# Ahead of layer 2 of a cross network: the second filter is loaded by SyncE and made into parts by VectorE, ScalarE does more of the first tile's stores and loads

## The reference

```python
for W in filters:                       # three layers, 128 outputs each
    b, f, d = x0.shape
    g = xk.shape[1]
    z = jnp.einsum('bfd,bgd->bfgd', x0, xk).reshape(b, f * g, d)
    cur = jnp.einsum('bpd,pm->bmd', z, W)
    outs.append(cur)
    xk = cur
result = jnp.concatenate(outs, axis=1)
z = jnp.sum(result, axis=-1)            # (512, 384)
h = jnp.concatenate([z, dense_ctx], axis=1)
h = jnp.maximum(h @ W_top1 + b_top1, 0.0)
h = jnp.maximum(h @ W_top2 + b_top2, 0.0)
y = h @ W_top3
```

## Time and profile before

| | us |
|---|---|
| median of 3 runs | 685.78 (683.43 to 687.0) |
| the profiled execution | 684.99 |
| its span in the profile | 683.0 |
| layer 2 of tile 0 begins, from the span's start | 48.48 |

### The profile page before, as it was taken

How to read it: one execution, slowest core, us unless ns; L and a number is a source line. 1 busy time by engine, 2 the same in 40 slices (tenths; PEclk the granted TensorE clock), 3 DMA queues, 4 the chain that set the end, 5 groups by cost and what they waited for, 6 DMA issues and landing times.

```text
span 683.0 us, 11480 instructions
## 1 busy us (share of the span) xinstructions
PE 642.6 (94%) x2942; PEld 510.8 (75%) x2942; DVE 564.9 (83%) x1914; ACT 383.4 (56%) x1157; POOL 532.2 (78%) x528
## 2 busy tenths in 40 slices
PE   3279999999999999999999999999999999999998
PEld 1156777767768787888868787888878888888867
DVE  4459897988989897989879897989879797988760
ACT  0447574746657574747467474746557474655431
POOL 6756989898999899897879989897959988574420
PEclk9989999999999999999999999999999999999998
DMA  9536533104040404013130404004040221200000
GB/s 185 92 93 232 151 74 92 30 8 116 10 116 8 116 9 116 6 26 98 31 94 6 116 9 110 13 8 115 7 115 7 63 62 36 82 1 1 1 1 0
DMA packets 70979, 41.92 MB, mean 61 GB/s; under 512 B 45889, under 2 KB 55761, under 8 KB 70786
## 3 DMA queue, kind: packets, MB, share of 16 engines
q1 hardware_dynamic: 58286, 35.53, 19.5%
q10 hardware_dynamic: 7380, 4.38, 3.1%
q0 software_dynamic: 5248, 1.29, 1.9%
HBM read 39.20 MB, written 1.94 MB: 60 GB/s over the span
## 4 chain that ended last, share of the span: by engine, by line
PE 73%; DVE 12%; issue 7%; POOL 3%; SPq 2%; ACT 2%; DMA 1%; DVEq 0%; POOLq 0%
PE y L853 18%; PE y L855 16%; PE y L854 16%; DVE scaled L756 10%; PE late L871 4%; PE side L860 4%; PE acc L835 3%; PE acc L829 3%; PE acc L830 3%; PE y L871 2%; ACT scaled L560 1%; PE late L882 1%; SPq L376 1%; POOL z_parts L463 1%; DVE z L717 1%
## 5 line engine op out<-in xcount | busy, mean ns | idle before, releaser
L756 DVE SCALAR_TENSOR_TENSOR scaled<-y,x_rows,scaled 128x128 f32<-128x128 f32 x1728 | 466.4, 343 | 71.2 <-ACT scaled L560 41.9
L560 ACT ACTIVATE scaled<-y,x_rows 128x128 f32<-128x128 f32 x768 | 218.3, 366 | 216.2 <-PE y L855 200.7
L853 PE MATMUL y<-w_hi,x_parts 128*128 128x512 f32 (+1 forms) x640 | 276.8, 432 | 6.8 <-DVE scaled L756 3.2
L855 PE MATMUL y<-w_hi,x_parts 128*128 128x512 f32 (+1 forms) x640 | 248.1, 388 | 0.0
L854 PE MATMUL y<-w_lo,x_parts 128*128 128x512 f32 (+1 forms) x640 | 247.4, 387 | 0.0
L463 POOL TENSOR_TENSOR z_parts<-z,z_parts 117x512 fp32r<-117x512 f32 (+1 forms) x107 | 138.4, 1294 | 33.4 <-ACT z_parts L514 32.5
L452 POOL DMA_INDIRECT emb_quads<-in_small_tables_dram,quad_rows x144 | 138.8, 964 | 27.2 <-issue 15.3
L853 PEld LDWEIGHTS y<-w_hi,x_parts 128*128 128x128 f32 x640 | 120.5, 188 | 44.7 <-DVE scaled L756 19.3
L855 PEld LDWEIGHTS y<-w_hi,x_parts 128*128 128x128 f32 x640 | 120.1, 188 | 25.0
L854 PEld LDWEIGHTS y<-w_lo,x_parts 128*128 128x128 f32 x640 | 121.0, 189 | 18.2
L478 POOL TENSOR_TENSOR sum<-sum,scaled 128x512 f32<-128x512 f32 x63 | 81.6, 1295 | 29.1 <-DVE scaled L756 28.3
(11 more groups left out here) (95 smaller groups left out, 360.2 us busy)
## 6 DMA issues: line engine op xcount, KB each, us to landing
z<-x_turned SPq DMA_DIRECT2D x311, 78.0 KB
x_three<-x_turned SPq DMA_DIRECT2D x48, 78.0 KB
x_turned<-emb_quads SPq DMA_DIRECT2D x156, 8.0 KB
w_sb<-in_w_dram SPq DMA_DIRECT2D x1, 2496.0 KB
emb_quads<-in_small_tables_dram,quad_rows POOLq DMA_INDIRECT x144
s_sb<-in_w_dram ACTq DMA_DIRECT2D x12, 160.0 KB
x_turned<-emb_singles SPq DMA_DIRECT2D x89, 2.0 KB
x_turned<-emb_quads SPq DMA_DIRECT2D x64, 2.0 KB
```

Of the source, the lines that this page charges most:

```text
L560: done = act.activation(scaled[:, k % 2, BY_ACT.index(j), i * M:(i + 1) * M], y2[n % RING][:, i * M:(i + 1) * M], ACT.Copy, scale=x0_rows[ ...
L756: dve.scalar_tensor_tensor(part, y2[n % RING][:, i * M:(i + 1) * M], x0_f, part, ALU.mult, ALU.add).then_inc(terms_in, 1)
L853: pe.matmul(dst, x1_hi[:, t % 2, cols], hi, start=True, stop=False)
L855: pe.matmul(dst, x1_lo[:, t % 2, cols], hi, start=False, stop=True).then_inc(y_ready, 1)
```

## The change

The edits all stand ahead of layer 2 of tile 0.

1. SyncE issues the 16 DMAs of the second filter, right behind its three loads of ids and numbers. Before, ScalarE issued them.
2. VectorE makes the second filter's high part itself, piece by piece, ahead of each low part. Before, ScalarE made it.
3. The stores of tile 0 are shared out anew. SyncE keeps 13 DMAs (five singles, quads 8, 4, 7, 0 and 5 in copy 0). ScalarE has the others of tile 0, and the six of tile 1's singles come first.
4. ScalarE issues `three` and chunks 0, 1, 2 and 4 of tile 0. SyncE issues chunks 3, 5 and 6 and `three_blocks`. Before, ScalarE had chunks 0, 3 and 5.
5. ScalarE's four activations on the dense part move from behind w0_hi to between the high parts of chunks 1 to 4. `three` is now a function of any queue, and ScalarE's copy is called `three_to_psum`.

```diff
--- before.py
+++ after.py
@@ -376,15 +376,22 @@
                     queue.dma_start(x0_dram[u, at:at + n, :].rearrange("f (b d) -> (f b) d", d=D),
                                     emb_quads[SPT * j:SPT * (j + n), u % 2, i, :]).then_inc(stored[u % 2], 16)
 
+        def three(queue, u):
+            if u >= 2:
+                queue.wait_ge(three_up, u - 1)
+                queue.wait_ge(rows_t, u - 1)
+            for r in range(3):
+                queue.dma_start(x0_three[F * r:F * r + F, u % 2, :], x0_dram[u, 0:F, :]).then_inc(three_in[u % 2], 16)
+
         block = ctx.enter_context(nc.Block())
 
         @block.sync
         def _(sp):
-            def stores(u, copies):
-                if u != 1:
-                    store_singles(sp, u, copies)
+            def stores(u):
+                if u > 1:
+                    store_singles(sp, u, (0, 1))
                 for i in QUAD_ORDER:
-                    store_quad(sp, u, i, copies)
+                    store_quad(sp, u, i, (0, 1))
 
             def three_blocks(u):
 
@@ -393,21 +400,22 @@
                 for k in range(3):
                     sp.dma_start(x0_stack[F * k:F * k + F, u % 2, :], x0_dram[u, 0:F, P * k:P * k + P]).then_inc(stack_in[u % 2], 16)
 
-            def three(u):
-                if u >= 2:
-                    sp.wait_ge(three_up, u - 1)
-                    sp.wait_ge(rows_t, u - 1)
-                for r in range(3):
-                    sp.dma_start(x0_three[F * r:F * r + F, u % 2, :], x0_dram[u, 0:F, :]).then_inc(three_in[u % 2], 16)
-
             sp.dma_start(ids_sb[:, 0, :], ids[0:P, :]).then_inc(ids_in, 16)
             sp.dma_start(table_number[:, 0, :], row_numbers[0:1, 0:SMALL].to_broadcast([P, SMALL])).then_inc(numbers_in, 16)
             sp.dma_start(ids_sb[:, 1:GROUPS, :], ids[P:B, :].rearrange("(g p) f -> p g f", p=P)).then_inc(rest_ids_in, 16)
+            for j in range(W1_PIECES):
+                load_filter(sp, j)
+            store_singles(sp, 0, (0,))
+            for i in (8, 4, 7, 0, 5):
+                store_quad(sp, 0, i, (0,))
             for u in range(TILES):
-                stores(u, (0,) if u == 0 else (0, 1))
-                sp.wait_ge(stored[u % 2], 16 * STORES * (u // 2 + 1))
-                three(u)
-                for c in (1, 2, 4, 6) if u == 0 else range(C0):
+                if u > 0:
+                    stores(u)
+                    sp.wait_ge(stored[u % 2], 16 * STORES * (u // 2 + 1))
+                    three(sp, u)
+                else:
+                    sp.wait_ge(stored[0], 16 * STORES)
+                for c in (3, 5, 6) if u == 0 else range(C0):
                     if u > 0:
                         n = C0 * (u - 1) + c
                         if low_by_dve(n):
@@ -530,7 +538,10 @@
                 act.activation(diag[at, t % 2, :, b, :], x0_rows[at, t % 2, :, :], ACT.Copy,
                                scale=mask_sb[at, b:b + 1]).then_inc(diag_in, 1)
 
-            def three(u):
+            def dense_part(c):
+                act.activation(dense_h1[:, c, :], y2[c][:, 0:LEFT], ACT.Identity, bias=bt1_sb[:, c:c + 1]).then_inc(dense_up, 1)
+
+            def three_to_psum(u):
                 act.wait_ge(three_in[u % 2], 48 * (u // 2 + 1))
                 if u > 0:
                     act.wait_ge(prod, C0 * u)
@@ -611,31 +622,26 @@
             act.dma_start(wt1_sb[0:16, 3, :], wt1[3 * P:FEATURES, :]).then_inc(dense_in, 16)
             act.dma_start(dense_sb[:, :], dense_t).then_inc(dense_in, 16)
             act.dma_start(bt1_sb[:, :], bt1).then_inc(dense_in, 16)
-            for j in range(W1_PIECES):
-                load_filter(act, j)
             act.wait_ge(w0_sum, 1)
             copy(w0_hi[:, :, :], w0_raw).then_inc(w0_hi_in, 1)
+            store_singles(act, 0, (1,))
+            store_singles(act, 1, (0, 1))
+            for i, copies in ((4, (1,)), (0, (1,)), (1, (0, 1)), (2, (0, 1)), (3, (0, 1)), (6, (0,))):
+                store_quad(act, 0, i, copies)
+            act.wait_ge(stored[0], 16 * STORES)
+            three(act, 0)
+            turned_rows(act, 0, 0)
+            turned_rows(act, 0, 1)
+            three_to_psum(0)
+            turned_rows(act, 0, 2)
             act.wait_ge(dense_in, 48)
             act.wait_ge(dense_ready, 1)
-            for c in range(H1 // P):
-                act.activation(dense_h1[:, c, :], y2[c][:, 0:LEFT], ACT.Identity, bias=bt1_sb[:, c:c + 1]).then_inc(dense_up, 1)
-            store_singles(act, 0, (1,))
-            for i in QUAD_ORDER:
-                if any(len(rows) > 1 for _, _, _, rows in runs(QUADS[i])):
-                    store_quad(act, 0, i, (1,))
-                if i == 0:
-                    store_singles(act, 1, (0, 1))
-            for j in range(W1_PIECES):
-                act.wait_ge(w1_in[j], 64)
-                copy(w1_hi[:, j:F:4, :], w1_raw[:, j:F:4, :]).then_inc(w1_hi_in, 1)
-            act.wait_ge(stored[0], 16 * STORES)
-            turned_rows(act, 0, 0)
-            three(0)
-            turned_rows(act, 0, 3)
             for c in range(C0):
                 high_part(0, c)
                 if c == 0:
-                    turned_rows(act, 0, 5)
+                    turned_rows(act, 0, 4)
+                elif c <= H1 // P:
+                    dense_part(c - 1)
             rows(0)
             x1_high(0)
             act.wait_ge(mask_in, 1)
...
@@ -767,7 +773,9 @@
                 dve.wait_ge(s_ready, k - 1)
                 dve.tensor_tensor(x2_sb[:, k % 2, :], sum2[:, 0:M], sum2[:, M:2 * M], ALU.add).then_inc(x2_in, 1)
 
-            def second_filter_low(i):
+            def second_filter_parts(i):
+                dve.wait_ge(w1_in[i], 64)
+                dve.tensor_copy(w1_hi[:, i:F:4, :], w1_raw[:, i:F:4, :]).then_inc(w1_hi_in, 1)
                 dve.wait_ge(w1_hi_in, i + 1)
                 dve.tensor_tensor(w1_lo[:, i:F:4, :], w1_raw[:, i:F:4, :], w1_hi[:, i:F:4, :].bitcast(F32),
                                   ALU.subtract).then_inc(w1_lo_in, 1)
@@ -788,7 +796,7 @@
             dve.wait_ge(w0_hi_in, 1)
             dve.tensor_tensor(w0_lo[:, :, :], w0_raw, w0_hi[:, :, :].bitcast(F32), ALU.subtract).then_inc(w0_lo_in, 1)
             for i in range(W1_PIECES):
-                second_filter_low(i)
+                second_filter_parts(i)
             for c in range(C0):
                 product(0, c)
                 if c > 0 and low_by_dve(c - 1):
```

More of the change, by code:

```diff
@@ L664, in _ @@
                     if t == 0 and s == FIRST_THREE_AT:
-                        three(1)
+                        three_to_psum(1)
                     if t + 2 < TILES and s == THREE_AT:
-                        three(t + 2)
+                        three_to_psum(t + 2)
                     if g > 0:
```

## The result

The change made the kernel slower, by 0.39%. The changed kernel takes 689.09 us (median of 11, 684.73 to 689.93), the one before 685.85 us beside it (median of 11), ratio 1.0039 [1.0022, 1.0056]. Measured again at the end it is 1.0033 [1.0007, 1.0060]. Forecast were 682.2 us and a range of 679.0 to 687.0. The profiled execution of after is the fastest of its 11 (684.73 us, span 682.7).

A forecast was written before the change was run, and what follows sets the result against it. TensorE is busy for 94% of the span, so only the ends can shrink. Gains of 1.3 us up to S and 2.3 us to layer 2 make 3.6 us: 681.4 profiled, 682.2 us forecast, range 679.0 to 687.0.

The forecast's parts named there:

- The second term: From S to layer 2 of tile 0: product 2 comes sooner, 2.3 us gained, ends 0.4 and 4.3 gained.
- S: Moment at which all stores of tile 0 have landed, 28.13 us in the profile before; forecast 26.9.
- The first product comes where it was: Behind S: the first product stays about 5.3 us behind S, as in the kernel before.
- The first term: Up to S: tile 0's stores land sooner, 1.3 us gained, ends 2.4 gained and 1.6 lost.
- an issue 3.3 us earlier: Filter on SyncE: the DMA engines are full anyway, so issuing 3.3 us earlier lets its data land hardly earlier.
- rival 2: Up to S: conversions lengthen the last four gathers of tile 0 by 1.1 us each; 685.5 us, chance 0.12.
- S': S in the changed kernel, when all stores of tile 0 have landed; forecast 26.9.
- rival 4: Up to S: SyncE's slow pace reaches the filter from its ninth DMA; S' 35.6, 690.9 us, chance 0.12.
- slow pace: SyncE needing 1.40 us per DMA, as for loads behind its quad stores in the profile before.
- rivals 3: At tile 1: SyncE's loads at 1.40 us make its stores late and all gain goes; 685.8 us, chance 0.08.
- Rival 1: From S to layer 2: TensorE's clock stays up, 4.3 us gained there; 680.2 us, chance 0.13.

The follow-up runs named there:

- f4: Changed kernel with the second filter issued by ScalarE and the first tile's loads shared out as before; ratio to the kernel before 0.9978.
- g5: Kernel before with only the new share-out of the first tile's loads (edit 4); ratio 1.0047.
- f1: Changed kernel with edit 1 alone undone, so ScalarE issues the second filter as before; ratio to the kernel before 1.0039.
- e3: Changed kernel, but SyncE starts its loads of chunks 3, 5, 6 and three_blocks only when three_in has landed; ratio to the kernel before 1.0053.
- g1: f1 with ScalarE's loads of chunk 2 ahead of its copy of three_ps, which waits for three_in; ratio to the kernel before 1.0050.
- h2: f1 with the three_in loads back on SyncE's queue; ratio to the kernel before 1.0042.
- f2: Kernel before with edit 1 alone, so SyncE issues the second filter; ratio 0.9981.
- e2: Changed kernel, but ScalarE makes the second filter's high parts between its stores and VectorE only the low parts; ratio to the kernel before 1.0055.
- e1: Changed kernel, but VectorE begins the second filter's parts only after the last gather of tile 0 has landed; ratio to the kernel before 1.0038.
- i2: Changed kernel measured again unchanged, on one chip with the kernel before; ratio 1.0033.
- groups e to h: Four of five groups of follow-up runs; each group shared one chip with runs of the kernel before, each group on another chip.
- h1: f1 with 20 instead of 12 filler matmuls behind S; ratio to the kernel before 1.0035.
- g4: Changed kernel with edit 4 alone undone, the first tile's loads shared out as before; ratio to the kernel before 1.0023.
- h3: f4 with 16 instead of 12 filler matmuls; ratio to the kernel before 0.9994.
- e4: Kernel before with edit 2 alone, so VectorE makes both parts of the second filter; ratio 0.9989.
- h4: e4 with 18 instead of 12 filler matmuls; ratio to the kernel before 0.9996.

## Why the prediction was wrong

**The second term was the step that failed** (from S to layer 2, 2.3 us gained). Its sentence "Chunk 2: issued behind, to 5.5, it is there at 8.1" assumed that a load lands 2.61 us after its issue, whatever else moves. In after chunk 2 was issued until S + 6.1 and was waited for until S + 10.8, 4.7 us behind the issue; chunk 0 was issued until S + 2.6 and came at S + 7.0. In the 4 us from 33 on the DMA engines were 92% busy:
```profile
33.00:37.00 4.00, 0.67 (x3) 0.19 (x2) 0.69 (x1) 0.73 (x2) 3.09 (x4) 0.86 0.92 229
```
In the first 8 us behind S the rows point to the order of the bytes. The DMA view of after, 29 to 37 us, ScalarE's queue and then SyncE's (packets, MB, share of 16 engines):
```profile
q10 hardware_dynamic: 516, 0.80, 37.2%
q1 hardware_dynamic: 695, 0.70, 37.0%
```
and of f4, 27 to 35 us:
```profile
q1 hardware_dynamic: 661, 1.02, 41.9%
q10 hardware_dynamic: 251, 0.40, 16.5%
```
SyncE's 0.70 MB of after begin with the eight loads of chunks 3, 5 and 6 (78 KB each, 0.62 MB), which nothing uses before S + 12. In f4 they are three_in and the chunks 1, 2, 4 in the order of use. Meanwhile ScalarE has six loads in a row ahead of product 0, and chunk 2 behind the wait for three_in. That edit 4 costs is shown by g5 against before and by f1 against f4, each pair on one chip. That it costs through this order is argued from the rows: e3, g1 and h2 each put one piece of it right and moved a product by 1.4 to 2.5 us, and none of them gained in the time. The distance fits: layer 2 - S is 20.5 to 21.8 us in all 12 profiles with the new share-out, and 17.3 to 19.4 us in the six with the old one other than before's own, whatever the filter, the conversions and the stores do. Before itself has 20.3 and 20.4; I put that down to SyncE's slow three_in loads, which no run tests. With the old share-out and SyncE at 0.38 us per load, layer 2 does come 1 to 3 us sooner behind S, as the second term had hoped; edit 4 pays that away. "The first product comes where it was" was wrong by 1.8 us for the same reason.

**The first term was wrong in its sign** (S at 26.9; measured 29.02 and 29.96). Four steps failed. The filter took SyncE 12.6 us instead of 10.3, 0.79 us each (this held nothing up, for the singles were not there yet). Tile 0's singles could be stored only at 15.0, by SyncE and ScalarE alike (before by SyncE at 12.56), and one quad gather took 3.28 us. f2 shows both with edit 1 alone (3.32 us, singles at 15.32). All eight profiles with the filter on SyncE have one gather of 3.28 to 3.54 us, none of the other twelve has. The prediction took "an issue 3.3 us earlier" for harmless; it costs what is beside it. And rival 2 came true as a mechanism: w0_hi was ready early, so VectorE's work fell on tile 0's gathers and stretched four to 1.8 to 2.0 us; quad 6 was issued until 26.17 instead of 20.14. The prediction had charged one such stretch of 1.1 us. The fourth step went the other way: it let quad 6's rows and its store take 2.6 us each to land, and in after S came only 2.85 us behind the end of that gather's issue, not 5.65. Rival 2, at 0.12, had S' at 30.2 and was the nearest to what came. The Trainium skill ("SBUF — State Buffer", section "Who interferes with whom") says that a cast can hold the port pair that VectorE shares with GpSimd, and that a tensor_tensor takes only the read side of it. The trace agrees as far as gathers took 1.8 to 2.0 us beside a conversion and its low part and 1.1 to 1.6 us beside low parts alone (e2). But the low parts were not harmless either, and in before one gather beside them took 2.04 us. A conversion alone was not measured. Still, e1 (no stretch, S 28.80) against f1 (no early filter, S 27.52), though on different chips, put more of the delay of S on the filter than on the conversions.

One sum of the prediction is off by 1 us and changes nothing: rival 4 with the slow pace from the first DMA on gives S' at 41.7 and so 697, not 698.

**Right** were the place (the two profiles part ahead of the end of layer 2 of tile 0 and then run in step up to tile 15), that the conversions have no direct cost (their price was taken as 1.3 us and measured as 0.81), products 3 to 6 not waiting, and the missing slow pace of SyncE: rivals 3 and 4 did not occur. Rival 1 did not either: the gap ahead of the first contraction grew from 2.13 to 3.88 us and the clock fell as before (at 0.50 for 6.8 us in both, from 34.8 in before and from 35.9 in after).

**The size.** Against the forecast, S is 2.1 us late and the way from S to layer 2 2.75 us long, together 4.9 us of the 6.8 us between the forecast change (-3.6) and the measured one (+3.2). Of the rest about 0.6 us stay open, and 1.3 us lie inside layer 2 of tile 0, where TensorE waits once more:
```profile
57.85 0.50 PE L861 MATMUL y<-w_hi,x_parts 128*128 128x512 f32 x1 [1.86 <-DVE scaled L762]
```
What VectorE waited for there is open. i2 has only 0.34 us of this wait, but its TensorE ran at half clock from 51.7 to 55.1 and again from 666.1 to 672.9:
```profile
51.70:55.10 3.40, 3.40 (x9) 2.65 (x9) 1.09 (x5) 1.75 (x6) 2.49 (x3) 0.50 0.64 163
666.10:672.90 6.80, 6.27 (x23) 4.89 (x23) 0.36 (x2) 0.75 (x2) 0.00 (x0) 0.50 0.01 2
```

**What the clock has to do with it.** The mean granted clock of every execution is known, and it shows what one profile per kernel can't. On the chips of groups e to h all kernels with the new share-out but h1 were granted less on average than before beside them, for example f1 0.9898 against 0.9934, g5 0.9919 against 0.9950, h2 0.9910 against 0.9950. Those with the old share-out were granted as much as before or more (f4 0.9948, g4 0.9956, h3 0.9958). What this is worth can be read from before itself on the chip of group h: its executions at 0.995 took 679.57 to 681.80 us, those at 1.000 took 677.34 to 678.56, so 0.005 of the mean clock is about 3 us, an estimate. By that estimate about 3 of the 4.7 us between f1 and f4 are time at half clock, and about 2 of the 2.8 us between g5 and before. The profiles show one place for it: four of the 12 with the new share-out (e1, e3, h2, i2) have a second drop of 3.4 us at 50.8 to 51.7, none of the eight others has. But it is not the whole loss. h1, with more fillers, was granted as much as before (0.9949 and 0.9950) and its ratio is still 1.0035. The same holds for i2 and before beside it (0.9903 and 0.9901, ratio 1.0033).

**Open.** Edit 1 without edit 4 is 0.9981 on one chip (f2) and with edits 2, 3 and 5 1.0023 on another (g4), so I can't say whether it costs in the time or only in S. Why before's three_in loads are slow is unknown, and whether they are on the chips of e4 and f2, where before was timed but not profiled. And f4, h3 and h4, whose layer 2 starts over 3 us ahead of before's profiles, measured only 0.0 to 0.2% below before on their own chips. Either before starts layer 2 earlier there too, or the gain is lost behind it; a profile of before on those chips would tell, and there is none. No version was measured faster than before beyond its interval.

## What to carry to other kernels

When loads are shared out over two queues, list them in the order in which they are needed and see that the bytes of the first microseconds of the stage go to the first users: a queue that is free is no reason to start what is needed last. A landing time read from one row holds only for the load on the DMA engines at that row: 2.6 us in the chain of before became 4.4 to 4.7 us at a share of 0.92. There, reckoning the bytes ahead of a load over the GB/s of the window would have been the better estimate, though no run here tests it. And a step taken off one engine's list moves all behind it: ask what it now lies beside.
